# Transposing the weighted low-rank activations on VectorE in 32x32 blocks, in an AdaLN feed-forward kernel on one Trainium2 core

## The reference

```python
out = jnp.einsum('boi,bih->boh', agg_w, x) + agg_b[:, :, None]      # conditioning
logits = x_flat @ W_router.T                                        # 8 experts
topk_probs, topk_idx = jax.lax.top_k(softmax(logits), 2)            # then normalised
combine = jnp.einsum('nk,nke->ne', topk_probs, onehot)
h = jnp.einsum('nd,erd->ner', x_flat, A)                            # 8 x 16 = 128 low-rank columns
hw = h * combine[:, :, None]
expert_out = jnp.einsum('ner,eor->no', hw, B) * 2.0
out = x_flat @ W_base.T + b_base + expert_out
```

## Time and profile before

| | before |
|---|---|
| median of 3 runs | 957.26 us (957.16 to 957.99) |
| the profiled execution | 956.88 us, of which the span from the first to the last instruction 955.2 us |
| mean granted TensorE clock | 1.000 |
| TensorE busy | 938.6 us (98%), 6705 matmuls |
| VectorE busy | 698.1 us (73%), 1555 instructions |
| ScalarE busy | 332.1 us (35%) |
| GpSimd busy | 87.0 us (9%) |
| DMA | 111.33 MB, mean 117 GB/s |

### The profile page before, as it was taken

One profiled execution on the slowest core, in us unless ns is written; L12 is line 12 of the kernel. 1 busy time (PEld: TensorE's weight loads), 2 busy tenths in 40 slices (PEclk: granted clock), 3 DMA queues, 4 the chain that ended last, 5 costly groups with the idle time before them and its releaser, 6 DMA issues.

```text
span 955.2 us, 18726 instructions
## 1 busy us (share of the span) xinstructions
PE 938.6 (98%) x6705; PEld 934.4 (98%) x6705; DVE 698.1 (73%) x1555; ACT 332.1 (35%) x663; POOL 87.0 (9%) x134
## 2 busy tenths in 40 slices
PE   5999999999999999999999999999999999999997
PEld 4999999999999999999999999999999999999997
DVE  4988777677777777777777777677767677767686
ACT  5553333333333333333333323333323333323431
POOL 0010100000100010101010101010101010101010
PEclk9999999999999999999999999999999999999999
DMA  7535434344434344434344434344434444444434
GB/s 268 176 68 136 112 114 125 101 125 100 112 113 119 105 119 104 112 113 113 111 113 107 115 114 109 114 107 107 118 116 105 119 103 106 120 120 104 120 90 110
DMA packets 35089, 111.33 MB, mean 117 GB/s; under 512 B 13024, under 2 KB 13408, under 8 KB 30592
## 3 DMA queue, kind: packets, MB, share of 16 engines
q1 hardware_dynamic: 25856, 77.55, 22.3%
q0 software_dynamic: 9216, 33.56, 21.2%
HBM read 75.37 MB, written 35.65 MB: 116 GB/s over the span
## 4 chain that ended last, share of the span: by engine, by line
PE 97%; DMA 1%; DVE 0%; issue 0%; SPq 0%; ACT 0%; DVEq 0%
PE ps L415 25%; PE ps L419 25%; PE ps L417 25%; PE ps L475 9%; PE ps L451 4%; PE ps L449 4%; PE ps L453 3%; DMA w_stage<-in_wide 1%; PE ps L498 1%; PE ps L441 0%; PE ps L442 0%; PE ps L501 0%; ACT w_hi L704 0%; DVE x_sb L1201 0%; SPq L356 0%
## 5 line engine op out<-in xcount | busy, mean ns | idle before, releaser
L415 PE MATMUL ps<-w_hi,x_hi 128*128 128x290 f32 x1552 | 463.5, 299 | 11.2 <-DVE w_lo L983 9.8
L417 PE MATMUL ps<-w_lo,x_hi 128*128 128x290 f32 x1552 | 460.7, 297 | 0.0
L419 PE MATMUL ps<-w_hi,x_lo 128*128 128x290 f32 x1552 | 459.8, 296 | 0.0
L415 PEld LDWEIGHTS ps<-w_hi,x_hi 128*128 128x128 f32 x1552 | 293.7, 189 | 13.2 <-issue 10.5
L419 PEld LDWEIGHTS ps<-w_hi,x_lo 128*128 128x128 f32 x1552 | 293.4, 189 | 0.0
L417 PEld LDWEIGHTS ps<-w_lo,x_hi 128*128 128x128 f32 x1552 | 293.4, 189 | 0.0
L666 ACT CAST x_hi<-xT_sb 128x512 fp32r<-128x512 f32 x186 | 115.6, 621 | 192.5 <-DVE xT_sb L902 165.9
L886 DVE TENSOR_TENSOR x_lo<-xT_sb,x_hi 128x512 fp32r<-128x512 f32 x186 | 127.4, 686 | 34.3 <-ACT x_hi L666 34.3
L863 POOL DMA_DIRECT2D x_sb<-in_x x64 | 56.4, 882 | 512.5 <-DVE x_sb L976 512.3
L962 DVE TENSOR_TENSOR hwT_lo<-ps,hwT_hi 128x128 fp32r<-128x128 f32 x64 | 18.7, 292 | 96.5 <-ACT hwT_hi L678 95.7
L681 ACT COPY sum<-ps 128x580 f32<-128x580 f32 x96 | 61.9, 645 | 63.3 <-PE ps L419 62.3
(11 more groups left out here) (115 smaller groups left out, 1105.1 us busy)
## 6 DMA issues: line engine op xcount, KB each, us to landing
x_sb<-in_x POOLq DMA_DIRECT2D x64, 512.0 KB, 5.4
result<-x_sb SPq DMA_DIRECT2D x63, 512.0 KB, 3.0
xT_sb<-in_xT SPq DMA_DIRECT2D x31, 1024.0 KB, 4.8
b_sb<-in_wide SPq DMA_DIRECT2D x2, 1160.0 KB, 13.2
agg_w_rows<-agg_w SPq DMA_DIRECT2D x1, 2048.0 KB, 7.5
mix<-agg_w_rows SPq DMA_DIRECT2D x124, 16.0 KB, 2.8
w_stage<-in_wide SPq DMA_DIRECT2D x2, 580.0 KB, 6.2
w_stage<-in_wide SPq DMA_DIRECT2D x1, 1160.0 KB, 11.5
```

The lines of the kernel that those rows point to most:

```text
L415: nc.tensor.matmul(dst, x_hi[:, s, rows], high[:, c, cols], start=first, stop=False, skip_group_check=True)
L417: nc.tensor.matmul(dst, x_hi[:, s, rows], low[:, c, cols], start=False, stop=False, skip_group_check=True)
L419: mm = nc.tensor.matmul(dst, x_lo[:, s, rows], high[:, c, cols], start=False, stop=last, skip_group_check=True)
```

## The change

`hwT` moves from PSUM to SBUF. TensorE's `transpose_hw` and its six calls go (64 transposes in all). VectorE gets a `transpose_hw` of its own: it waits for `hw_done` and issues 16 transposes of 32x32 blocks, block (i, j) of `hw` to block (j, i) of `hwT`, each raising `hwT_made` by one. It stands right behind `route` in each place where VectorE routes a tile. `hwT_high` on ScalarE now waits for all 16 of them, and also for the experts of the tile before (`out_mm`; for the last tile `last_piece_mm`). The remaining order of all engines stays.

```diff
+BLOCK, BLOCKS = 32, 4
-O_BANK, T_BANK = 4, 7
+O_BANK = 4
...
+        hwT = sb("hwT", [P, P])
-        hwT = ps[:, T_BANK, 0:P]
...
-            def transpose_hw(u, side):
-                pe.wait_ge(hw_done, tile_no(u, side) + 1)
-                nc.tensor.transpose(hwT, hw[:], ident).then_inc(hwT_mm, 1)
...
                 product_part(b, "A12", 0, True)
-                transpose_hw(u - 1, 0)
                 product_part(b, "A12", 1, True).then_inc(product_mm, 1)
...
                 product_part(a, "S3", 0, False)
-                transpose_hw(u - 1, 1)
                 product_part(a, "S3", 1, False).then_inc(product_mm, 1)
...
-            def hwT_high(u, side):
-                act.wait_ge(hwT_mm, tile_no(u, side) + 1)
-                nc.scalar.copy(hwT_hi[:], hwT).then_inc(hwT_hi_done, 1)
+            def hwT_high(u, side, experts_done=out_mm, before=None, first=False):
+
+                act.wait_ge(hwT_made, (tile_no(u, side) + 1) * BLOCKS * BLOCKS)
+                if not first:
+                    act.wait_ge(experts_done, tile_no(u, side) if before is None else before)
+                nc.scalar.copy(hwT_hi[:], hwT[:]).then_inc(hwT_hi_done, 1)
...
+            def transpose_hw(u, side):
+
+                dve.wait_ge(hw_done, tile_no(u, side) + 1)
+                for i in range(BLOCKS):
+                    for j in range(BLOCKS):
+                        there, here = slice(j * BLOCK, (j + 1) * BLOCK), slice(i * BLOCK, (i + 1) * BLOCK)
+                        nc.vector.transpose(hwT[there, here], hw[here, there]).then_inc(hwT_made, 1)
...
                 z21_low(u - 1, b)
                 route(u - 1, 0)
+                transpose_hw(u - 1, 0)
                 x_low(u, "S2")
                 z22_low(u - 1)
                 hwT_low(u - 1, 0)
...
                 route(u - 1, 1)
+                transpose_hw(u - 1, 1)
                 hwT_low(u - 1, 1)
```

More of the change, by code:

```diff
@@ L242, in build @@
         hw_done = sem("hw_done")
-        hwT_mm = sem("hwT_mm")
+        hwT_made = sem("hwT_made")
         hwT_hi_done = sem("hwT_hi_done")
@@ L643, in _ @@
             mixed(1, 0, LAST_BANKS[0], last_z_hi, last_z_lo).then_inc(ar_mm, 1)
-            transpose_hw(u, 0)
             pe.wait_ge(z22_summed, u + 1)
@@ L658, in _ @@
             mixed(1, 2, LAST_BANKS[2], last_z_hi, last_z_lo)
-            transpose_hw(u, 1)
             for k in range(PIECES):
@@ L783, in unit @@
                 x_high("S3")
-                hwT_high(u - 1, 0)
+                hwT_high(u - 1, 0, first=first)
                 if first:
@@ L846, in _ @@
             gate(u, 1)
-            hwT_high(u, 1)
+            hwT_high(u, 1, last_piece_mm, 2)
         @block.gpsimd
@@ L958, in route @@
                     expert_w[:].unsqueeze(2).to_broadcast([P, EXPERTS, RANK]), ALU.mult, ALU.mult).then_inc(hw_done, 1)
+            def transpose_hw(u, side):
[4 more added lines that the diff above has]
+                        nc.vector.transpose(hwT[there, here], hw[here, there]).then_inc(hwT_made, 1)
             def hwT_low(u, side):
                 dve.wait_ge(hwT_hi_done, tile_no(u, side) + 1)
-                nc.vector.tensor_tensor(hwT_lo[:], hwT, hwT_hi[:].bitcast(F32), ALU.subtract).then_inc(hwT_lo_done, 1)
+                nc.vector.tensor_tensor(hwT_lo[:], hwT[:], hwT_hi[:].bitcast(F32), ALU.subtract).then_inc(hwT_lo_done, 1)
             def result(u, side):
@@ L1063, in unit_1 @@
                 route(0, 0)
+                transpose_hw(0, 0)
                 x_low(1, "S2")
@@ L1076, in unit_1 @@
                 route(0, 1)
+                transpose_hw(0, 1)
                 x_low(1, "S4")
@@ L1169, in _ @@
             route(u, 0)
+            transpose_hw(u, 0)
             dve.wait_ge(p5_saved, u)
@@ L1196, in _ @@
             route(u, 1, LAST_BANKS[0])
+            transpose_hw(u, 1)
             def add_piece(side, k, bank):
```

## The result

The changed kernel takes 1092.08 us (median of 6 runs, 1089.4 to 1094.1) against 957.3 us of the kernel before: a ratio of 1.1407, interval 1.1393 to 1.1420. It is slower by 135 us. The forecast was 1065.6 us, with 1024 to 1116 as its range. The profiled span is 1089.8 us, with a mean granted TensorE clock of 0.967 in place of 1.000.

A forecast was written before the change was run, and what follows sets the result against it. TensorE, busy 98%, bounded the old kernel; VectorE would bound the new one. Thirty turns, each 3.24 us longer (+97.2), and end terms made +108.3: span 955.2 to 1063.5, run 1065.6 us, range 1024 to 1116.

The forecast's parts named there:

- T: Time VectorE needs for the 16 block transposes of one tile: forecast 3.68 us, bounds 3.04 to 4.32.
- the sum: Whole kernel: 30 longer turns (+97.2 us) and the terms at the end, together +108.3 us, giving 1065.6 us.
- What goes: 64 transposes leave TensorE at 0.11 to 0.12 us each: 28.50 us for a unit, 7.2 us in all.
- The price of a block: Start-to-start distance of VectorE's 32x32 transposes, taken from the two copies into `agg_b`: 0.23 us each.
- rival 1: VectorE's block transposes overlap, 0.11 us each; TensorE stays the bound and the kernel takes 953.6 us; chance 0.12.
- VectorE's turn: VectorE's cycle from `hw` to `hw` over one two-tile unit: 31.96 us against TensorE's 28.50, so VectorE becomes the bound.
- the formula: Length of VectorE's cycle over one unit: 24.60 + 2T us.
- Stretch (a): First tile on VectorE, from `hw` to the result's first add: 4.60 us becomes 3.17 + T.
- stretch (b): Second tile on VectorE, from `hw` to `z_lo`: 3.99 us becomes 1.30 + T.
- The store's wait: VectorE's 0.98 us idle ahead of the next unit's S2; the store follows the result, so it moves along.
- Behind the turns: Last unit and last tiles: +2.1 and -0.2 at the first experts, +2.7 second experts, +3.2 S4, +3.3 last tile.
- rival 3: TensorE's granted clock falls to 1.2 GHz after each unit's waits: 50 us in all, 1116 us; chance 0.05.

## Why the prediction was right, and where it was off

The direction and the main mechanism held: VectorE became the bound, by twice T a unit. The term that is missing from the sum is the granted clock. How close the rest of the sum comes is in part luck.

- **What goes.** 0.11 us a transpose held: with both tiles off TensorE and VectorE quick enough, units are 28.5 us (the same-partition kernel), with one tile 28.6.
- **The price of a block**, the step that had no row. 0.23 us was taken from the one pair of instructions on different partitions, and 0.234 was measured. The experiment with unchanged partitions, 0.096 us, even less than the 0.11 of rival 1, supports the reason as well. The Trainium skill's rule in "VectorE: DVE Perf Modes", section "Two Vector instructions with no wait between them", agrees with the traces on both sides: output in the changed kernel, input with the loops exchanged. Strictly, by that rule fifteen of the sixteen are held and the instruction behind them, not all 16: the first block begins where `hw` begins.
- **VectorE's turn.** With T = 3.74 the formula gives 32.1 us; the turns with full clock are 31.7 to 32.1 (one is 32.9), and 31.9 in the mean over all 30 where TensorE is kept busy. Stretch (a) was to be 3.17 + T = 6.91 and is 6.93, stretch (b) 1.30 + T = 5.04 and is 5.06. The store's wait moved along: 0.86 us before L893 at 514.78, 0.98 before.
- **Behind the turns.** The last S2 to the end was to grow by 11.1 us and grew by 15.4 (39.7 to 55.1 us). The waits fit. TensorE's waits after, from 1030 us to the end:

```profile
PE ps L477 <- ACT hwT_hi L673: 4.3, 2, 2.3
PE ps L493 <- ACT hwT_hi L673: 3.9, 1, 3.9
PE ps L417 <- DVE sum L900: 3.7, 1, 3.7
```

  They are the first and the second experts', the last experts' (0.4 before) and S4's (0.3 before), against a sum of 2.1, 2.7, 3.3 and 3.2: they grew by 11.2 us, where these terms make 11.3. That leaves some 4 us. The windows behind the last S2, of the changed kernel, of the one with the busy TensorE and of the kernel before, have a granted clock of 0.86, 0.87 and 1.00:

```profile
1034.70:1089.80 55.10, 39.11 (x232) 37.08 (x230) 41.01 (x143) 10.87 (x25) 3.53 (x5) 0.86 0.27 67
...
1010.50:1064.20 53.70, 40.04 (x244) 38.08 (x242) 40.82 (x143) 10.76 (x25) 3.57 (x5) 0.87 0.28 69
...
915.50:955.20 39.70, 34.66 (x239) 33.57 (x237) 28.05 (x79) 10.83 (x25) 3.54 (x5) 1.00 0.38 93
```

  By an estimate from the 0.86, some 15 us of this stretch ran at half the clock. That can account for the 4 us, but no run shows its price there apart.
- **The step that was mis-sized: the clock.** It stood among the rivals as rival 3 with 0.05, at 50 us, and not in the sum. It came, in 17 of 30 turns, and filling the waits gave back 26 us. Treating it as a case that excludes the others was the fault: a forecast of 2.9 us of waiting in each unit made it a term of the forecast itself. TensorE's wait for `hwT_hi` was 2.2 us, where some 2.5 had been forecast (and 2.9 used in the sum for all of the first experts' waiting), and the few short waits of the kernel before had given no reason either to expect or to exclude it.

The sum without the clock, 1065.6, is close to what the kernel with the busy TensorE takes, 1066.2, but that is in part luck. In that kernel the 30 turns are 2.8 us shorter than the sum has them (957.3 against 862.9 + 97.2) and the stretch behind them is 2.9 us longer (53.7 against 39.7 + 11.1). With the measured T of 3.74, the same sum would have given 3.8 us more.

## What to carry to other kernels

An engine at 73% has 27% to give only if its idle time stands where the new work goes: here the same sixteen instructions cost 0.3 us a unit in one place and 2.0 us in the other. Count the new engine's own cycle from a step to the same step of the next round, with every wait that would vanish taken out and every store that hangs on it left in, and compare it with the old bound. Then ask apart from that what the old bound will wait for: with only the first tile on VectorE, VectorE had 2.8 us of idle time left in each unit, and the kernel still took 1023.65 us, where the rival by VectorE's turn alone had 955. And many small VectorE instructions that move between groups of partitions cost a little more than their full duration each (0.234 us apart at 0.203), where the same ones on unchanged partitions overlap (0.096 apart at 0.159).

## What was not expected of the hardware

- In the changed kernel TensorE waited 1.9 to 2.5 us for the first experts of every unit. In 17 of 30 turns the granted clock was 0.50 for 3 to 4 us afterwards, in the others it stayed at 1.00 after waits of the same length. With only the first tile on VectorE it fell twice, after waits of 2.5 and 2.4 us, and from 200 to 900 us, with waits up to 1.6 us in each unit, it stayed at 1.00.
- More work can be less time: 372 matmuls in the waits, whose result nobody reads, saved 26 us.
- A 32x32 transpose lasts 0.203 us in the mean where its partitions differ from those of the last, and 0.159 us where they don't; not only the overlap, the duration changes too.
